# A fused scan, attention and expert kernel: unpadded queries, an f32r bias product, merged routing and a new order of operations

## The reference, cut to what matters

```python
x = x + mamba(_layernorm(x))          # projections, convolution, a scan over the 1024 tokens
x = x + experts(_layernorm(x))
x = x + attention_and_mlp(_layernorm(x))
x = x + experts(_layernorm(x))        # the same expert weights again
...
def step(s, t):                       # the scan: state of 256 x 32 per batch
    s = jnp.clip(s * A + b_t[:, None, :] * x_t[:, :, None], -10.0, 10.0)
    y = jnp.sum(c_t[:, None, :] * s, axis=-1)
...
phi_q = relu(q) + 0.001; phi_k = relu(k) + 0.001      # 16 heads of width 16
out_i = phi_q_i . cumsum_j<=i phi_k_j v_j^T / (phi_q_i . cumsum phi_k_j)
...
scores = xf @ gate_w + gate_b         # 8 experts, top 2
comb = zeros_like(scores).at[rows, topk_i].add(topk_s)
h = maximum(einsum('nd,edh->neh', xf, w1) + b1, 0)
out = einsum('ne,ned->nd', comb, einsum('neh,ehd->ned', h, w2) + b2)
```

## Time and profile before

| | |
|---|---|
| time, median of 3 runs | 2015.1 us (2014.0 to 2020.18) |
| the profiled execution | 2020.32 us, span from first to last instruction 2018.5 us |
| PE busy | 1890.2 us, 94% of the span |
| DVE busy | 1596.6 us, 79% |
| ACT busy | 514.7 us, 25% |
| POOL busy | 231.8 us, 11% |
| granted TensorE clock, mean | 0.959 of full speed |

### The profile page before, as it was taken

The page is one execution under the profiler, slowest core; times in us unless marked ns, Lnnn a source line. Parts: engine busy times, 40 slices in busy tenths (PEclk is TensorE's granted clock), DMA queues, the critical chain, the costliest instruction groups (busy, mean ns, idle before and its releaser), DMA issues. The chain is left out here.

```text
span 2018.5 us, 58331 instructions
## 1 busy us (share of the span) xinstructions
PE 1890.2 (94%) x18240; PEld 1595.4 (79%) x18240; DVE 1596.6 (79%) x6197; ACT 514.7 (25%) x1120; POOL 231.8 (11%) x514
## 2 busy tenths in 40 slices
PE   6775688999999999999999999999999999999997
PEld 3443477888888888888888888888888888888886
DVE  4557887888888888888888888888888888887432
ACT  4341012222221313232222222131323222222222
POOL 0001101011010102020101111110202010110100
PEclk9885598999999999999999999999999999999998
DMA  6852010100010010101010001000010101010000
GB/s 233 270 149 55 13 28 14 29 20 24 15 33 14 21 27 14 29 18 29 20 28 20 24 16 31 14 23 25 17 30 16 29 20 28 20 29 8 1 7 6
DMA packets 100871, 72.98 MB, mean 36 GB/s; under 512 B 64744, under 2 KB 94448, under 8 KB 99568
## 3 DMA queue, kind: packets, MB, share of 16 engines
q1 hardware_dynamic: 98272, 67.54, 11.6%
q10 hardware_dynamic: 2320, 1.85, 0.3%
HBM read 45.74 MB, written 23.59 MB: 34 GB/s over the span
## 5 line engine op out<-in xcount | busy, mean ns | idle before, releaser
L1557 DVE CUSTOM_DVE_ANT_0 state<-decayed_state,bank 128x128 f32<-128x128 f32 x2048 | 507.2, 287 | 83.0 <-PE bank L1094 72.0
L1547 DVE TENSOR_TENSOR decayed_state<-state,decay 128x128 f32<-128x128 f32 x2048 | 517.8, 293 | 9.0 <-issue 6.8
L1193 PE MATMUL bank<-f_w_sb,hs_whole 128*128 128x256 f32 x2048 | 489.0, 382 | 0.0
L1193 PEld LDWEIGHTS bank<-f_w_sb,hs_whole 128*128 128x128 f32 x2048 | 373.9, 190 | 49.8 <-ACT hs_whole L987 5.3
L987 ACT ACTIVATE hs_whole<-bank,f_b_sb 128x256 f32<-128x256 f32 x512 | 214.1, 469 | 695.7 <-PE bank L1180 695.6
L1094 PE MATMUL bank<-xrows,brows 128*128 128x256 f32 x1024 | 261.1, 345 | 44.5 <-DVE state L1557 33.0
L1094 PEld LDWEIGHTS bank<-xrows,brows 128*128 128x128 f32 x1024 | 175.2, 199 | 94.9 <-issue 56.0
L1180 PE MATMUL bank<-late_fT_parts,f_w_hi 128*128 128x256 f32 x1024 | 179.3, 298 | 0.5 <-ACT hs_whole L987 0.5
L1180 PE MATMUL bank<-fT_parts,f_w_hi 128*128 128x256 f32 x1024 | 166.7, 288 | 0.0
L1180 PEld LDWEIGHTS bank<-late_fT_parts,f_w_hi 128*128 128x128 f32 x1024 | 143.8, 192 | 15.6 <-issue 11.5
L1675 DVE SCALAR_TENSOR_TENSOR x<-bank,comb,x 128x256 f32<-128x256 f32 x256 | 111.8, 479 | 52.3 <-PE bank L1193 50.6
(11 more groups left out here) (155 smaller groups left out, 2420.6 us busy)
## 6 DMA issues: line engine op xcount, KB each, us to landing
brows<-bs_dram SPq DMA_DIRECT2D x1020, 2.0 KB
xrows<-xs_dram SPq DMA_DIRECT2D x480, 32.0 KB
xt<-in_x SPq DMA_DIRECT2D x4, 1024.0 KB, 7.8
xn_dram<-xn SPq DMA_DIRECT2D x4, 1024.0 KB, 5.4
z_dram<-zT SPq DMA_DIRECT2D x4, 1024.0 KB, 4.1
f_w_sb<-in_f_w SPq DMA_DIRECT2D x2, 2048.0 KB
xs_dram<-xhi SPq DMA_DIRECT2D x4, 1024.0 KB, 5.2
xs_dram<-xlo SPq DMA_DIRECT2D x4, 1024.0 KB, 8.4
```

The source lines that it names most:

```text
L1193: last = pe.matmul(bank_[:, tile * D:(tile + 1) * D], hs_whole[:, slot, m, tile * P:(tile + 1) * P], w(m), start=(m == 0 and tile == 0 and ...
L1547: dve.tensor_tensor(decayed_state[:, part], state[:, (s - 1) % RING, part], decay[:, part], ALU.mult).then_inc(decayed.sem, 1)
L1557: dve._custom_dve(add_sat, out=state[:, s % RING, part], in0=decayed_state[:, part], in1=U[s // 2 % 2][:, s % 2 * D + h * HALF:s % 2 * D + ...
```

## The change

- Queries: `wq` is no longer padded ([256, 256]), the query product is one call with two groups, and both halves of `qT` are made from the same bank: `max(q, floor) + eps`, where for the head that isn't this half's `floor` is the largest float and `eps` its negative, so that the sum is zero.
- Bias: `comb` is written three times into a 128-column tile at columns 0, 32 and 64 (rounded to f32r twice, and the rest that rounding left), and `f_b2` into rows 0, 32 and 64 likewise (high, low, high). One f32r product over 128 rows for each tile takes the place of the f32 product over 8. The transpose and its copy now cover 128 rows.
- Routing: each operation takes both tiles at once, the threshold and the multiplication are one instruction, and two small instructions fill the stacked tile.
- Set-up: two more fills on POOL, three small loads on SP behind a wait, one rounding on ACT and one subtraction on DVE for `f_b2`.
- Order: the step is written in another order on PE, DVE, ACT and POOL.

Cut to its core:

```diff
-        wq = weight("wq", [P, KD, GROUPS * P])
+        wq = weight("wq", [P, KD, KGROUPS * P])
...
+            sp.wait_ge(pool_set.sem, POOL_SETS)
+            for n in range(3):
+                sp.dma_start(g["f_b2"][SLOT * n:SLOT * n + E, :], t["f_b2"]).then_inc(g["back_in"], 16)
...
                 rstd_of(late, FFN2)
+                rstd_of(c, OUTER)
                 next_cblk(1)
                 next_cblk(2)
+                rstd_of(c, LN1)
+                add_mlp_bias()
                 next_cblk(3)
...
                 relu(c, 0, 1)
-                copy_comb(c, 0)
                 ln_apply(late, FFN2, x3, late_turn, xf_done[1])
+                copy_comb(c, 0)
...
                 copy_set(c, T_ATT)
+                copy_v(c)
                 relu(late, 1, 3)
-                copy_v(c)
...
+                spread_kv(c)
                 copy_hi(c, T_MLP)
-                spread_kv(c)
...
-                        last = pe.transpose(TB[0:E, tile * P:(tile + 1) * P], comb[:, f, tile, :], ident[:])
+                        last = pe.transpose(TB[:, tile * P:(tile + 1) * P], comb_rows[:, tile, :].bitcast(f32), ident[:])
...
-                                         g["f_b2"][:], start=True, stop=True)
+                                         b2_rows[:], start=True, stop=True)
...
-                def features(w, j, made):
-                    for gr in (2 * j, 2 * j + 1):
+                def features(w, made):
+                    for gr in range(KGROUPS):
                         for k in range(KD):
-                            last = pe.matmul(NB[j][:, gr % 2 * TOK:(gr % 2 + 1) * TOK], w[:, k, gr * P:(gr + 1) * P],
+                            last = pe.matmul(HB[1][:, gr * TOK:(gr + 1) * TOK], w[:, k, gr * P:(gr + 1) * P],
...
+                    dve.tensor_tensor(ge, f_, e_, ALU.is_equal).then_inc(route[f].sem, 1)
+                    dve.tensor_tensor(gt, f_, e_, ALU.is_gt).then_inc(route[f].sem, 1)
+                    dve.wait_ge(route[f].sem, route[f].after(c, 2))
+                    dve.tensor_tensor(level[:], level[:], g["before"][:].unsqueeze(1).broadcast_to([P, TILES, E * E]), ALU.mult).then_inc(route[f].sem, 1)
+                    dve.wait_ge(route[f].sem, route[f].after(c, 4))
+                    dve.tensor_tensor(above[:], above[:], level[:], ALU.add).then_inc(route[f].sem, 1)
+                    dve.wait_ge(route[f].sem, route[f].after(c, 5))
+                    dve.tensor_reduce(rank[:], gt, AX.X, ALU.add).then_inc(route[f].sem, 1)
+                    dve.wait_ge(route[f].sem, route[f].after(c, 6))
+                    dve.scalar_tensor_tensor(out=comb[:, f], in0=rank[:], scalar=1.5, in1=score[:], op0=ALU.is_lt, op1=ALU.mult).then_inc(comb_done[f].sem, 1)
+                    dve.wait_ge(comb_done[f].sem, comb_done[f].after(c, 1))
+                    slots = comb_rows[:].rearrange("p i (r x) -> p i r x", x=SLOT)
+                    dve.tensor_copy(slots[:, :, 0:2, 0:E], comb[:, f].unsqueeze(2).broadcast_to([P, TILES, 2, E])).then_inc(comb_done[f].sem, 1)
+                    dve.wait_ge(comb_done[f].sem, comb_done[f].after(c, 2))
+                    dve.tensor_tensor(slots[:, :, 2, 0:E], comb[:, f], slots[:, :, 0, 0:E].bitcast(f32), ALU.subtract).then_inc(comb_done[f].sem, 1)
...
+                def query_feature(half):
...
+                    dve.wait_ge(q_made.sem, q_made.after(c, 1))
+                    dve.tensor_scalar(qT[:, KGROUPS * half:KGROUPS * (half + 1)].rearrange("p k q -> p (k q)"), HB[1][:],
+                                      g["feature_floor"][:, half:half + 1], g["feature_eps"][:, half:half + 1],
+                                      ALU.max, ALU.add).then_inc(qT_done.sem, 1)
```

More of the change, by code:

```diff
@@ L1368, in step @@
                 u(0)
+                u(1)
+                turn_y()
+                mlp_second(0)
+                mamba()
                 mlp_first(late, 1)
-                turn_y()
-                u(1)
-                mlp_second(0)
-                u(2)
-                mamba()
-                u(3)
-                mlp_second(1)
-                mlp_first(late, 2)
+                u(2)
+                mlp_first(late, 2)
+                mlp_second(1)
+                u(3)
                 mlp_first(late, 3)
@@ L1420, in step @@
                 second_layer(c, 0, 6)
+                bias(late, 1)
                 u(15)
@@ L1459, in step @@
                 turn_k()
-                u(23)
-                u(24)
+                second_layer(late, 1, 4)
+                y(4)
                 pe.wait_ge(qT_done.sem, qT_done.after(c, 2))
@@ L1646, in routing @@
-                    for n, step in enumerate(steps):
-                        for tile in range(TILES):
-                            e_ = score[:, tile].unsqueeze(2).broadcast_to(grid)
-                            f_ = score[:, tile].unsqueeze(1).broadcast_to(grid)
-                            gt = above[:, tile].rearrange("p (e f) -> p e f", e=E)
-                            ge = level[:, tile].rearrange("p (e f) -> p e f", e=E)
-                            if n >= 2:
-                                dve.wait_ge(route[f].sem, route[f].after(c, 1 + TILES * (n - 1) + tile + 1))
-                            step(tile, e_, f_, gt, ge).then_inc(comb_done[f].sem if n == 6 else route[f].sem, 1)
+                    grid = [P, TILES, E, E]
@@ L1786, in step @@
                 add_expert(c, 0, 0, res)
+                scan(16, 18)
                 add_expert(c, 0, 1, res)
-                scan(16, 17)
+                scan(18, 19)
+                add_expert(c, 0, 2, res)
+                scan(19, 22)
                 routing(late, 1)
-                scan(17, 19)
-                add_expert(c, 0, 2, res)
-                scan(19, 21)
                 add_expert(c, 0, 3, res)
-                scan(21, 26)
-                set_acc(late, 1, x3, x3)
-                scan(26, 27)
+                scan(22, 24)
@@ L1797, in step @@
                 add_expert(c, 0, 4, res)
-                scan(27, 28)
+                scan(24, 26)
+                low_half(late, T_FFN2)
+                scan(26, 29)
                 add_expert(c, 0, 5, res)
-                scan(28, 29)
-                low_half(late, T_FFN2)
+                scan(29, 30)
                 add_expert(c, 0, 6, res)
-                scan(29, 30)
+                scan(30, 32)
                 add_expert(c, 0, 7, res)
                 ln_stats(c, OUTER, res, acc_done[0], (TILES * (E - 1) + 1, TILES * E))
-                scan(30, 32)
+                scan(32, 33)
@@ L1807, in step @@
                 ln_apply(c, OUTER, res, a_t, a_done)
+                scan(33, 34)
                 ln_stats(c, LN1, a_t, a_done, (1, 2))
[L1809 removed]
+                set_acc(late, 1, x3, x3)
+                scan(34, 35)
                 ln_affine(LN1, a_t, "ln1_s", lambda tile: rows["ln1_b"][:], turn, xl_done)
[L1811 removed]
+                scan(35, 36)
                 add_expert(late, 1, 0, x3)
[L1813 removed]
+                scan(36, 38)
                 add_expert(late, 1, 1, x3)
[L1815 removed]
@@ L1828, in step @@
                 mask(2)
-                scan(48, 50)
+                scan(48, 49)
                 mask(3)
-                scan(50, 51)
+                scan(49, 51)
                 add_expert(late, 1, 5, x3)
@@ L1866, in lay_out @@
     order = [H // KGROUPS * a + PADH // DH * slot + half for half in range(PADH // DH) for a in range(KGROUPS) for slot in range(GH)]
-    def padded(w):
-        w = np.asarray(w)
-        full = np.zeros((D, PADH // DH, H * DH // PADH, PADH // DH, DH), w.dtype)
-        for half in range(PADH // DH):
-            full[:, half, :, half] = w[:, half::PADH // DH]
-        return blocks(full.reshape(D, H * PADH))
     a = {k[len("L0_"):]: np.asarray(v) for k, v in x.items()}
```

194 lines of the change are left out of this document (98 added, 96 removed).

## The result

The changed kernel takes 1932.26 us in the median (1931.47 to 1935.1), the kernel before 2016.38 us in its runs beside it. The ratio is 0.958 (95% interval 0.955 to 0.960), 84 us less. A later measurement of the same kernel gave 0.958 again (0.956 to 0.961).

A forecast was written before the change was run, and what follows sets the result against it. The prediction took PE, almost always busy in the loop, as the bound. Fourteen periods at -4.6 us (-64) with set-up, chunk 1 and drain made -70.5 us, from a median of 2015.1 to 1945 us, range 1935 to 1970.

The forecast's parts named there:

- What bounds the kernel: Loop: PE is busy 1397.25 of 1418.20 us, so PE savings shorten the time; DVE has 14.57 us a period spare.
- rival 4: Loop: DVE sets the pace once its forced waits pass 14.4 us (about 10 found); slower, 2061 us; chance 0.05.
- Queries, -1.73 us: PE, each chunk: one of two query product calls goes, saving 1.73 us.
- Bias and transposes, -1.76 us a period: PE: f32r bias products for 8-row f32 ones save 1.82 us a chunk; larger transposes of comb add at most 0.06.
- Routing, +0.1 us on DVE and nothing on PE: Expert routing: the merged eight-instruction chain takes about 1.9 us against 1.79, from -0.3 to +0.7, covered by PE work.
- Order, -0.9 us: PE, each period: new order removes 1.18 us of waits and adds 0.3 of stall; from -1.3 to +2.5.
- 0.3 us of new stall: PE, each period: allowance for hand-offs that come near in the new order.
- the three named waits: PE, each period: waits for normalised tokens (0.48 us), copied keys (0.39) and the MLP input's low half (0.31) go.
- rival 3: PE's residual idle time and half the hand-over gaps also go: -0.6 us a period, 1934 to 1938 us; chance 0.07.
- The hand-offs that come near: New order: masks stall 0.1 to 0.2 us, GELU up to 0.1; scores behind expert 4 and y7 have little slack.
- The ends, -6.5 us together: Outside the loop: set-up +0.5 us, chunk 1 -3 us, drain -4 us.
- The sum and the range: Period falls 4.6 us to 104.5, fourteen give -64, with ends -70.5 us: 1945 us, range 1935 to 1970.

The follow-up runs named there:

- order alone: Changed kernel with two padded query products, 8-row f32 bias product and old routing put back; ratio 0.986 against the kernel before, period 107.0 us.
- the y7 experiment: Kernel before with y(7), the scan's last output product, moved ahead of mlp_first(0) on PE; ratio 1.011, period alternating between 110.0 and 111.5 us.
- the first profile: Profiled execution of the changed kernel: 1935.1 us, with a loop period of 103.22 us.
- the second: The changed kernel measured once more, unchanged: 1931.24 us, ratio 0.958 against the kernel before, period 103.24 us.
- the queries alone: Kernel before, old order kept, with the second query product and its wait removed; ratio 0.991, period 108.0 us but for one of 111.8.

## Why the prediction was right and wrong, point by point

- *What bounds the kernel.* Right. PE was busy throughout the loop, and it alone gave the time back. DVE's waits fell from 14.57 to 9.4 us a period ("about 10"); rival 4, slower, had nothing for it.
- *Queries, -1.73 us.* Right in the new order: order alone and the changed kernel differ by the 1.72 us of its rows. In the old order they give 1.07.
- *Bias and transposes, -1.76 us a period.* Measured 2.16 in the old order and 2.1 in the new, too small by 0.3 to 0.4. The step that failed is the sum of gaps for the 8-row product. It counted the 0.09 us ahead and missed the one behind. The earlier trace rows show the start of a second layer (1016.07); the block behind it, which the prediction didn't read on to, is

```profile
1017.90 0.60 PE L1127 MATMUL bank<-ident_sb,late_turn 128*128 128x128 f32 x4
```

so that the layer took 1.83 us, where one behind full-array products takes 1.72. That is 0.2 us a period; 0.06 more is the transposes, which cost nothing. The remaining 0.1 in the old order is other waits that shifted.
- *Routing, +0.1 us on DVE and nothing on PE.* Right. The eight instructions run from 978.82 to 980.73 us, 1.91 us where 1.9 was worked out, and the 14 of the kernel before took 1.79.
- *Order, -0.9 us.* Measured -2.0 on its own: this is the term that was mis-sized, by 1.1 us a period, 15 us in all. Three parts. The 0.3 us of new stall that I added came to 0.05. Of the idle time I had only the three named waits go, 1.18 us; the rest went too, and it was 0.30 and not 0.43 us, as the window of the earlier trace rows took in some drain (rival 3 had priced the residue and half of the gaps at 0.6 with a chance of 0.07). The step that failed by most is the price of a wait: I took each at its recorded idle time. From start to start the four are worth 0.63 (tokens, recorded 0.47), 0.58 (keys, 0.39), 0.73 (low half, 0.30 or 0.39) and 0.45 (GELU, 0.19), together 2.4 us for the 1.44 that the period of the earlier trace rows has as idle. By the order alone 0.6 of that excess reached the period. I had read waits from their idle column and blocks from start to start, though front and prediction said that recorded ends are modelled and overlap.
- *The hand-offs that come near.* All held: scores, masks, `y7`, GELU. Where one doesn't, the price is seen in the y7 experiment: the same edit without DVE's part of the order loses 1.6 us a period.
- *The ends, -6.5 us together.* Measured -3.4 in the first profile and -7.3 in the second (chunk 0 with the front +1.2, chunk 1 -2.4, the drain -6.1). The second is near what was worked out; between them lies the scatter of front and chunk 1. The drain gave 6.1 to 6.5 us instead of 4. But the kernels with `y(4)` or `y(7)` moved, which have the drain's work unchanged, took 3.0 and 4.8 us less for it than the kernel before (153.40 and 151.62 us against 156.39), and the order alone 1.5 more (157.85). So the drain of one execution can't carry a reading of 2 us. The granted clock over those drains was 0.96 and 0.98 against 0.93, with 0.94 for the order alone and 0.96 in the changed kernel. Whether clock or hand-offs carry the difference was not tried.
- *The sum and the range.* The terms of a period sum to -4.4 (1.73 + 1.76 + 0.9); I took -4.6 and had no term for the 0.2, which by luck hid a part of the error: the terms were 1.45 us a period short and the forecast 1.25. The range ended 3 us too high. The order's own bounds reached to -1.3; the sum had no bound for waits that are worth more than recorded, and that alone was 0.6 us a period.

Together: fourteen periods at 5.85 us instead of 4.6 are 17.5 us more, and that is more than the 14.7 us by which the forecast missed the first profile (1949.8 less 1935.1), with the chance delay of the front and chunk 1 making up the difference. What is settled is the split into bias (2.1), order (2.0) and queries (1.7). That the order gives 0.6 us more than idle time fits the waits read from start to start, which are worth 1.0 more than recorded. The 0.3 to 0.4 us between the two would be changes of shape that the new order adds, which I haven't taken apart; and of the four waits only those for the keys and the low half were taken away by edits of their own, each of which brought a new wait; the other two are read from rows alone.

## What to carry to other kernels

Where one in-order engine is full, price everything from start to start, the waits too: in each of the six waits read here (the four, the ReLU of the queries alone and the masks) the recorded idle time was less than the wait cost, by 0.1 to 0.4 us. Check too that a window doesn't reach out of the stretch that it is to stand for. A block that is taken out of such a queue may have been another hand-off's cover, and a swap in one queue may need its counterpart in the next; so an edit and the order around it are one change and should be forecast and tried as one. Work that must stay can be made cheaper by giving it the shape of its neighbours, even when it then has more rows.

## What the runs showed of the hardware that I had not expected

A product over 8 rows of the array costs more than the same over 128: 0.43 against 0.23 us for two of 256 columns in f32r, and 0.08 to 0.10 us more in the block on either side. The same twelve f32r products, behind and ahead of the same neighbours, take 1.69 us without a wait and 2.42 with one recorded as 0.30. And the front part, with the same instructions in the kernels before, with `y(7)` or `y(4)` moved and with the order alone, ended anywhere from 154.0 to 159.8 us, which is as much as many a change is worth.
